# Causal attention in the last stage: all row maxima in two halves of the TensorE array, operands in three rotating buffers, a written-out TensorE order, maxima rows issued by ScalarE

## The reference, cut to what matters

```python
x = L0_attn_x                                   # (16, 1024, 256)
xn = layernorm(x)
x = x + latent_attention(xn, ...) + lora_ffn(xn, ...)
xn = layernorm(x)
# L1 attention: 16 heads of 16, causal, with a linear position bias per head
q, k, v = heads(xn @ q_w + q_b), heads(...), heads(xn @ kv_w + kv_b)
att = q @ k.T / 4 + slope[head] * (key - query)
att = softmax(where(causal, att, -inf))
x = x + (att @ v) @ o_w + o_b + time_mix_ffn(xn)
```

## Time and profile before

| | |
|---|---|
| median of three runs | 2727.81 us (2725.26 to 2729.4) |
| the profiled execution's own time | 2729.97 us |
| its span in the trace | 2727.9 us |
| mean granted TensorE clock | 0.978 of full speed |
| `prepare` and `project` | up to 870.7 us |
| `attend` | 870.7 to 2727.9 us |

### The profile page before, as it was taken

One profiled execution on the slowest core, in us unless ns is written; L12 is line 12 of the kernel. 1 busy time (PEld: TensorE's weight loads), 2 busy tenths in 40 slices (PEclk: granted clock), 3 DMA queues, 4 the chain that ended last, 5 costly groups with the idle time before them and its releaser, 6 DMA issues.

```text
span 2727.9 us, 57513 instructions
## 1 busy us (share of the span) xinstructions
PE 2598.3 (95%) x21670; PEld 1637.9 (60%) x21670; DVE 2321.1 (85%) x4175; ACT 2059.8 (76%) x3887; POOL 1373.4 (50%) x1768
## 2 busy tenths in 40 slices
PE   6779999999997999999999999999999999999998
PEld 4569989999996444545445454454544545455454
DVE  3468888888886998999989998899998999999993
ACT  2248878877884687888887887788887887887886
POOL 2235555555653365464654645546464464654644
PEclk9889999999998899999999999999999999999999
DMA  2015575545555646556474564655546556474540
GB/s 73 1 44 171 179 189 186 173 164 177 176 178 165 106 74 123 80 99 106 73 127 75 104 105 68 122 82 98 100 79 122 82 97 102 77 127 77 103 89 17
DMA packets 315172, 299.58 MB, mean 110 GB/s; under 512 B 97174, under 2 KB 265516, under 8 KB 314668
## 3 DMA queue, kind: packets, MB, share of 16 engines
q1 hardware_dynamic: 313344, 295.55, 50.9%
q10 hardware_dynamic: 1552, 0.36, 0.1%
HBM read 175.27 MB, written 120.06 MB: 108 GB/s over the span
## 4 chain that ended last, share of the span: by engine, by line
PE 54%; ACT 6%; DMA 5%; issue 1%; SPq 0%; DVE 0%; POOL 0%; POOLq 0%; ACTq 0%
PE t_y L1570 19%; PE t_r L1554 16%; PE t_a L1505 12%; ACT t_prob L1599 6%; DMA scr_m<-t_mrows 4%; PE t_a L1538 4%; PE t_r L1516 3%; DMA t_q<-scr_m 1%; DMA t_k<-t_blockb 0%; DVE t_mxc L1647 0%; ACT t_mrows L1616 0%; SPq L1411 0%; ACT t_near L1608 0%; SPq L1417 0%; POOL t_prob L1744 0%
## 5 line engine op out<-in xcount | busy, mean ns | idle before, releaser
L1599 ACT ACTIVATE t_prob<-t_r 128x512 f32<-128x512 f32 (+1 forms) x2432 | 1261.4, 599 | 289.5 <-PE t_r L1554 285.4
L1647 DVE TENSOR_REDUCE t_mxc<-t_a 128x1 f32<-128x512 f32 (+3 forms) x1920 | 1129.3, 643 | 105.4 <-PE t_a L1505 102.7
L1554 PE MATMUL t_r<-t_q,t_k 109*128 109x128 bf16 (+4 forms) x4608 | 831.7, 275 | 31.1 <-DMA t_q<-scr_m 20.9
L1505 PE MATMUL t_a<-t_k,t_q 99*128 99x512 bf16 (+3 forms) x2560 | 650.1, 320 | 1.5 <-DVE t_mxc L1647 1.0
L1750 POOL TENSOR_SCALAR_AFFINE_SELECT t_near<-t_near 128x512 f32<-128x512 f32 x512 | 332.7, 650 | 532.3 <-ACT t_near L1608 532.1
L1570 PE MATMUL t_y<-t_prob,t_v 128*32 128x512 f32 (+3 forms) x6144 | 588.0, 496 | 0.0
L1554 PEld LDWEIGHTS t_r<-t_q,t_k 102*128 102x128 bf16 (+1 forms) x4608 | 373.6, 98 | 342.9 <-ACT t_prob L1599 133.1
L1744 POOL TENSOR_SCALAR_AFFINE_SELECT t_prob<-t_prob 128x512 f32<-128x512 f32 x512 | 322.5, 637 | 276.9 <-ACT t_prob L1599 276.9
L1608 ACT COPY t_near<-t_r 128x512 f32<-128x512 f32 x512 | 307.5, 602 | 82.6 <-PE t_r L1516 65.6
L1505 PEld LDWEIGHTS t_a<-t_k,t_q 99*128 99x128 bf16 x2560 | 210.8, 98 | 228.5 <-DVE t_mxc L1647 155.0
L1570 PEld LDWEIGHTS t_y<-t_prob,t_v 128*32 128x32 f32 x6144 | 157.7, 109 | 257.3 <-issue 182.4
(11 more groups left out here) (199 smaller groups left out, 4129.2 us busy)
## 6 DMA issues: line engine op xcount, KB each, us to landing
t_q<-scr_q SPq DMA_DIRECT2D x384, 128.0 KB, 4.0
t_k<-scr_k SPq DMA_DIRECT2D x384, 128.0 KB, 6.6
scr_q<-j_part SPq DMA_DIRECT2D x96, 256.0 KB, 3.4
scr_k<-j_part SPq DMA_DIRECT2D x96, 256.0 KB, 2.5
scr_v<-j_v SPq DMA_DIRECT2D x32, 544.0 KB, 5.0
t_v<-scr_v SPq DMA_DIRECT2D x64, 272.0 KB, 8.1
p_x<-in_x SPq DMA_DIRECT2D x32, 512.0 KB, 4.3
scr_res<-j_x SPq DMA_DIRECT2D x32, 512.0 KB, 3.8
```

The costliest lines, as they stand in the source:

```text
L1505: mm = pe.matmul(abank[n % A_BANKS][:, x * w:(x + 1) * w], q_op[t % NG][0:KA, h0 + x, i * P:(i + 1) * P], k_op[t % NG][0:KA, h0 + x, k0:k0 ...
L1554: mm = pe.matmul(ring[n % RING_BANKS][:, s * w + lo:s * w + hi], k_op[g][0:deep, h0 + s, j * P:(j + 1) * P], q_op[g][0:deep, h0 + s, q0 + ...
L1599: nc.scalar.activation(prob[:, q % SLOTS, h0:h0 + m, 0:w], ring[n % RING_BANKS][:, 0:m * w].rearrange("p (h n) -> p h n", h=m), ACT.Exp).t ...
L1647: V.tensor_reduce(mxc[:, t % 2, k0 // 512, h0:h0 + m, i], abank[n % A_BANKS][:, 0:m * w].rearrange("p (h n) -> p h n", h=m), AX.X, ALU.max ...
```

## The change

**Maxima.** All of them, those on the diagonal too, are computed from operand buffers of their own, `t_qm` and `t_km`. Two of the group's four heads lie on partitions 0 to 63 and two on 64 to 127: three rows of position, three products of 16 rows instead of six, and 12 rows of marks that make future keys of the diagonal block very negative (contraction of 51 rows, 63 on the diagonal). Every matmul is issued twice, once for each half of the array's rows, each half writing a PSUM bank of its own. A unit fills two banks (`t_a`, now two buffers of 1024 columns; the `exp` ring goes from four banks to three) and VectorE reduces both with one instruction. A group has 19 units instead of 30 and 8. `keep`, `future` and `reduce` are gone, and one of the two joining instructions.

**Order.** `CYCLE` lists what TensorE does in one period of the steady state, each entry with how many periods it lags; `plan` follows it, and keeps its simulation for the other engines only.

**Buffers.** `q_op`, `k_op`, `v` and the new pair rotate over three sets. The queries and keys for the maxima are loaded separately (`load_maxima`: 14 DMAs a group beside 14 of `load_operands`), each in pieces (`keys`, `load`) placed in SyncE's queue by the plan's time.

**Maxima rows.** ScalarE issues the write (behind its copy) and the read back (`spread`), which before stood in SyncE's queue.

**Smaller parts.** The scaling after `invert` moves from VectorE to GpSimd. The residual loads and `shift` are placed later. The marks are built by GpSimd at the end of its part of `prepare` (46 fills, four selects, two copies).

```diff
+Q_MAIN = (0, 0, 1)
+K_MAIN = (0, 1, 0)
...
+def load_marks(eng, a, scr, q, k, done):
+    each = lambda t: t.rearrange("p (o n) -> p o n", o=1).to_broadcast([MSUB, GH // 2 * QT, P])
+    for e in range(2):
+        tiled = lambda t: t[64 * e + NMAIN:64 * e + NMAX, :, :].rearrange("p h (i n) -> p (h i) n", n=P)
+        eng.dma_start(k[64 * e:64 * e + NPOS, :, :], a["k_pos"][:, 0:GH // 2, :]).then_inc(done, 16)
+        eng.dma_start(tiled(q), each(scr["t_markq"][:, :])).then_inc(done, 16)
+        eng.dma_start(tiled(k), each(scr["t_markk"][:, :])).then_inc(done, 16)
...
+def load_maxima(eng, a, scr, q, k, t, done, e):
+    b, g = divmod(t, NG)
+    mine = slice(g * GH + e * GH // 2, g * GH + (e + 1) * GH // 2)
+    eng.dma_start(q[64 * e:64 * e + NPOS, :, :], a["q_pos"][:, mine, :]).then_inc(done, 16)
+    for op, src, parts in ((q, parts_of(scr, "qs"), Q_MAIN), (k, parts_of(scr, "ks"), K_MAIN)):
+        for n, s in enumerate(parts):
+            at = 64 * e + NPOS + n * HD
+            eng.dma_start(op[at:at + HD, :, :], src[s, b][:, mine, :]).then_inc(done, 16)
...
+                load_marks(sp, a, scr, qm0, km0, s_qk0)
+                load_constants(sp, a, scr, q0, k0, s_qkv0)
                 sp.wait_ge(s_q_out, 96)
...
+                for e in range(2):
+                    load_maxima(sp, a, scr, qm0, km0, 0, s_qk0, e)
+                for piece in range(LOAD_PIECES):
+                    load_operands(sp, a, scr, q0, k0, v0, 0, s_qkv0, piece)
...
-A_BANKS, RING_BANKS, SLOTS = 3, 4, 6
+A_SLOTS, RING_BANKS, SLOTS = 2, 3, 6
+BUFS = 3
+CYCLE = (
+    ("weigh", 1, 6), ("exp", 19, 6), ("exp", 20, 6), ("max", 8, 4), ("exp", 21, 6), ("out", 0, 7), ("out", 2, 8),
...
+    ("exp", 14, 5), ("exp", 15, 5), ("weigh", 0, 5), ("rows", 0, 4), ("exp", 16, 5), ("exp", 17, 5),
+    ("exp", 18, 5), ("max", 3, 3), ("max", 5, 3),
+)
...
+                for h in pair:
+                    for i, k0, w, near in pieces:
+                        far = w - P if near else w
+                        for depth, lo, hi in ((NMAIN, 0, far), (NMAX, far, w)):
+                            if lo < hi:
+                                for e in range(2):
+                                    mm = pe.matmul(abank[n % A_SLOTS][:, 512 * e + at + lo:512 * e + at + hi],
+                                                   q_max[t % BUFS][64 * e:64 * e + depth, h, i * P:(i + 1) * P],
+                                                   k_max[t % BUFS][64 * e:64 * e + depth, h, k0 + lo:k0 + hi],
+                                                   start=True, stop=True)
+                        at += w
...
-                    sp.dma_start(scr["m"][g], mrows[:, :]).then_inc(s_mw, 16)
-                    sp.wait_ge(s_mw, 16 * (t + 1))
-                    sp.dma_start(q_op[g][KA:KB, :, :].rearrange("p h t -> p (h t)"),
-                                 scr["m"][g].rearrange("(s n) q -> s (n q)", s=3)).then_inc(s_m[g], 16)
...
+                act.wait_ge(s_al, t + 1)
+                act.dma_start(scr["m"][t % NG], mrows[:, :]).then_inc(s_mw, 16)
+
+            def spread(t):
+                act.wait_ge(s_mw, 16 * (t + 1))
+                if t >= BUFS:
+                    act.wait_ge(s_pv, NQ * (t - BUFS + 1))
+                act.dma_start(q_op[t % BUFS][KA:KB, :, :].rearrange("p h t -> p (h t)"),
+                              scr["m"][t % NG].rearrange("(s n) q -> s (n q)", s=3)).then_inc(s_m[t % BUFS], 16)
```

More of the change, by code:

```diff
@@ L99, in prepare @@
         ones = sb("p_ones", [P, P])
+        marks = [sb(f"p_mark_{n}", [MSUB, P]) for n in "qk"]
         ldT = sb("p_ldT", [100, 4])
@@ L1174, in settle, with cyclic @@
                 e[4](end)
+def cyclic():
+    order = []
+    for period in range(min(e[2] for e in CYCLE), GROUPS + max(e[2] for e in CYCLE)):
+        for place, (kind, x, late) in enumerate(CYCLE):
+            t = period - late
+            if 0 <= t < GROUPS and (kind != "out" or t % NG == NG - 1):
+                order.append((period + place / len(CYCLE), kind, t // NG if kind == "out" else t, x))
+    return order
 def plan():
-    lead, lag = 1.5, 0.12
     pl = Planner()
-    width = [KEY_QUADS[r][3] * per_bank(KEY_QUADS[r][3]) for r, h0 in PIECES]
@@ L1183, in plan @@
-    at = [sum(width[:x]) / sum(width) for x in range(NP_ + 1)]
-    load = [n * w + 65 for i, k0, w, h, n in MAX_UNITS]
-    way = [sum(load[:u]) / sum(load) for u in range(NU + 1)]
     mm = lambda w: 4 + 0.42 * w
-    streams = {"max": [], "exp": [], "weigh": [], "out": [], "diag": []}
-    for t in range(GROUPS):
-        streams["max"] += [(t - lead + way[u], "max", t, u) for u in range(NU)] + [(t - lead + 1.12, "rows", t, 0)]
-        streams["diag"] += [(t - lead - 0.25 + 0.9 * i / QT, "diag", t, i) for i in range(QT)]
-        streams["exp"] += [(t + at[x], "exp", t, x) for x in range(NP_)]
-        streams["weigh"] += [(t + at[FIRST_PIECE[r // 2 * 2 + 2]] + lag, "weigh", t, r) for r in range(NQ)]
-        if t % NG == NG - 1:
-            streams["out"] += [(t + (1.0 if 2 * h < OUTS else 1.25) + 0.12 * h, "out", t // NG, h) for h in range(OUTS)]
@@ L1309, in plan @@
                 weighted(t, LAST_QUAD.index(x), now + 180)
-            if x == NQ - 1 and t + NG < GROUPS:
-                pl.order["SP"].append(("load", t, 0))
+            if x == NQ - 1 and t + BUFS < GROUPS:
+                pl.issue += [(now + 3000 * z, "load", t, z) for z in range(LOAD_PIECES)]
         elif kind == "out":
@@ L1314, in plan, with last @@
             slot_freed.append(("sum", t, x))
-            last = lambda end, t=t: pl.order["SP"].append(("store", t, 0))
+            def last(end, t=t):
+                pl.issue.append((end, "store", t, 0))
+                if t + 1 < B:
+                    residual(t + 1, end + 6000)
             pl.give("DVE", now + 165, rank, ("sum", t, x), 616, last if x == OUTS - 1 else None, "slot")
     pl.settle(pl.FAR)
+    pl.order["SP"] = [e[1:] for e in sorted(pl.issue)]
     return pl.order
@@ L1578, in _ @@
                     largest(t, x, slot[e])
-                elif what == "diag":
-                    on_diagonal(t, x, turn[e])
                 elif what == "rows":
```

411 lines of the change are left out of this document (199 added, 212 removed).

## The result

The changed kernel takes 2694.51 us (median of 4 runs, 2682.6 to 2696.55); the kernel before took 2728.61 us beside it. The ratio is 0.9862, 95% interval 0.9826 to 0.9898: 1.4% faster, where 4.9% was forecast, and outside the range.

The account below looks back on a forecast made before the run. TensorE was taken to bound `attend`, VectorE close behind; 870.7 before it + 9 `project` + 35 ramp + 63 steps of 25.85 + 51 end gave 2594.3 us span, median 2594 us, 4.9% less; range 2550 to 2680.

Parts of the forecast that it names:

- Waits: TensorE's waits in each group step of `attend`: 1.7 us before, bounds 0.4 and 1.7, taken as 0.9 us.
- ScalarE stalls behind its own write: Rival: exponentials queue behind the maxima write's landing, ScalarE stands 3 us a group, 2783 us; chance 0.04 in full.
- a partial stall: Mixture of a partial ScalarE stall at the write and late loads: 2660 to 2730 us, chance 0.05.
- Once a batch is not every group: Argument against ScalarE's stall: the write landed in 7.3 us behind the residual loads, which come only once a batch.
- Halves beside each other: Maxima matmuls on TensorE: both row halves run at once, 3.98 us a group instead of 7.97.
- rival of weights one after the other: Rival: halves' weights load in turn, 1.1 us a group over 20 pairs of 128 columns, 2663 us; chance 0.15.
- Changes of division: TensorE's switches of array division: 38.3 a group instead of 13.1, at 0.095 us each, +2.4 us.
- rival of cheap divisions: Rival: new division changes cost little, at most 0.95 us a group gained, put at 2545 us; chance 0.08.
- The reductions: VectorE's maxima reductions: 15 over 1024 columns at 1.15 us, 4 over 768 at 0.89, together 20.8 us a group.
- `project`: Group 0's loads in SyncE's queue: 18 DMAs become 38, costing +9 us (0 to 12).
- Ramp: Start of `attend` to first transpose: 32 us for 29 `max` units plus about 3 to start and split, 35 us.
- End: Time after the last transpose in `attend`: 51 us, against 47.4 before.

## Why the prediction was wrong

*The step that failed* is "Waits": "those for the read back go if ScalarE's write lands in time". It did not land in time. The text put six to nine exponentials between write and read back; that was right. It took 4.1 to 6.1 us for them, at the pace of 0.68 us that a group step gives; but ScalarE does such a stretch nearly back to back, and the work between was 3.5 to 5.7 us, 4.6 in the median. The landing took 5.9 us in the median and was longer in 63 of 64 groups. The term for all waits was taken as 0.9 us a group, with 1.7 as its upper bound; it was 2.5. With the read back placed later, and nothing else, it is 25.98 - 24.95 = 1.03. The prediction's own sign of being wrong, "if ScalarE stands idle for DMA", is what the trace showed.

*Its cause* stood among the rivals, "ScalarE stalls behind its own write", with 0.04 in full, and a partial stall within "2660 to 2730", in a mixture with 0.05. The measured 2694.51 us lie in that mixture. Two reasons were given against it. "The loads go through SyncE's queue, the write now through another": the landing shows that a queue of its own does not shield this write while the DMA engines are full, and it fell to 2.8 us only when the loads went away. "Once a batch is not every group": the earlier trace rows was read as a residual load's doing, but the operand loads of every group (1.8 MB) are nearly as large as the two residual loads (2 MB), and the changed kernel places them just ahead of the write, as the prediction itself says. The numbers to see it were there: a landing of 1.4 to 8.7 us against a room of 4.1 to 6.1. A wait whose range of before covers its room is a likely cost, not one of 4 in 100.

*Its size* was between nothing and the rival's 3 us a group, and its price was one us of time for about one us of stall, as the rival took it. With the read back placed later, ScalarE's idle time in the steady part falls by 96.7 us (502.4 to 405.7; window less busy time), 1.53 us a group, and the step by 1.47. On TensorE that came in two main parts: 0.93 us a group of idle time and 0.43 of the clock that falls behind it.

*What held.* Halves beside each other (3.98 us of columns): yes. The rival of weights one after the other: no, 0.06 us a pair. Changes of division at 0.095 us in full: yes, 0.32 us now and 0.31 before, against 0.22 without one. So the rival of cheap divisions falls as well. The Trainium skill, TensorEngine Tiling, Key Properties, has the change of mode drain the engine, and this trace agrees for halves of the rows too, with those 0.32 us. The Trainium skill's rule of some 4 ns for a further tile of a pack (TensorE: Matmul & The Clock Gate, Measured speedup vs the span model) agrees with the 3 ns here. The reductions, by busy time as they were forecast: 1.20 and 0.93 us (895.4 / 749 and 233.6 / 251), where 1.15 and 0.89 were computed and 1.205 stood as the upper bound; with 20.8 us a group counted, some 21.6 came. VectorE had 24.0 us a group (1514.35 / 63) instead of 22.9, and with the wait gone is busy 92% of the step, not 89%. It stayed below TensorE all the same. `project`: +9 forecast, +8.1 measured. Ramp 31.4 against 35: the 29 `max` units were reduced at VectorE's pace, as said, with 31.25 of 31.40 us busy; the 3 us for the start and the split did not come on top. End 51.4 against 51. The sum with the wait gone is 2606 us, 12 above the forecast, so the work that the change moves was read rightly and one wait wrongly. That the total came so close has a little luck in it: VectorE's term was 1 us a group too small, which did not show, since it is not the bound.

## What to carry to other kernels

Before a DMA issue with a wait is moved into the queue of an engine that computes, compare the whole range of that wait in the trace with the work that stands between, at every group; if the range covers it, place the waiting instruction as late as the longest landings (here 7 us of the plan were nearly enough for landings up to 9), which costs nothing as long as the data is not needed; here 10 us cost nothing either. Count the room by what the engine does back to back, not by the pace of the whole step. In this kernel the write's landing followed what SyncE's queue had under way, so look at SyncE's order ahead of it, not only at its own queue. And when a change gives far less than the work that it removes, look for an engine's idle time with a releaser that was not in the trace before: here it was one number away from being gone.

## What the runs showed of the hardware that was not expected

- Two matmuls on different halves of the array's rows, with different operands and banks, run wholly beside each other, their weight loads too: a step of 0.226 us for 2 x 512 columns, 0.32 with a change of division, and 0.055 us for 2 x 128.
- The write of the maxima rows (24 KB) lands after 1.4 us at the least, and after 5.9 us (median), up to 9.2, where SyncE's queue issues 13 operand loads just ahead of it, and after 2.8 us (median) where they are moved away.
- Stalls of ScalarE of 2 to 3 us go with a lower granted clock of TensorE: 0.78 and 0.73 in the two windows of 7 us at and behind one, and 54.6 us at the lower level in the steady part, in stretches that follow TensorE's gaps of 1.4 to 3.2 us. With the wait gone no gap behind 965 us is longer than 0.32 us, and no such stretch is left. Of the 92.9 us that the wait cost, some 27 were the clock's. In `project` a lowered clock is also seen behind the 38 loads (0.70).
